# A mixture of experts whose rows are summed in DRAM by accumulating DMAs, and a second residual and layer norm done by halves

## The reference

```python
x = x + tanh(g_xattn[0]) * L0_xattn(layernorm(x), ctx)
x = x + tanh(g_ffn[0])   * L0_ffn(layernorm(x))
x = x + tanh(g_xattn[1]) * L1_xattn(layernorm(x), ctx)
x = x + tanh(g_ffn[1])   * L1_ffn(layernorm(x))

def L0_ffn(x):                      # a transformer layer with experts
    x = x + self_attention(rms(x) ...) @ wo
    h = rms(x, ff_ln_w)
    topv, topi = top_k(h @ wg, 4)   # of 16 experts
    weights = zeros.at[topi].set(softmax(topv))
    a = silu(h @ w1[e]) * (h @ w3[e])
    return x + sum_e weights[:, e] * (a @ w2[e])

def L1_xattn(x, y):                 # 16 heads of 32
    q = ln(x @ Wq + bq); k = ln(y @ Wk + bk); v = y @ Wv + bv
    ...                             # softmax(q k) v, and the same on the last 16 keys
    return ctx @ Wo + bo
```

## Time and profile before

| | |
|---|---|
| median of 3 runs | 2946.0 us (2941.17 to 2949.18) |
| the profiled execution | 2944.19 us, its span 2942.4 us |
| PE busy | 2398.4 us, 82% |
| DVE, ACT, POOL busy | 1768.0, 1472.8, 1100.9 us |
| mean granted clock of TensorE | 0.926 of full speed |
| DMA | 194.94 MB, mean 66 GB/s |

### The profile page before, as it was taken

One profiled execution on the slowest core, in us unless ns is written; L12 is line 12 of the kernel. 1 busy time (PEld: TensorE's weight loads), 2 busy tenths in 40 slices (PEclk: granted clock), 3 DMA queues, 4 the chain that ended last, 5 costly groups with the idle time before them and its releaser, 6 DMA issues. The chain is left out here.

```text
span 2942.4 us, 46079 instructions
## 1 busy us (share of the span) xinstructions
PE 2398.4 (82%) x14790; PEld 1995.1 (68%) x14790; DVE 1768.0 (60%) x3807; ACT 1472.8 (50%) x3030; POOL 1100.9 (37%) x1497
## 2 busy tenths in 40 slices
PE   5999999999957998899885649889860689999355
PEld 3778787878756888888873548888860577777232
DVE  3555555555554666666666625454535688888576
ACT  3444444444435666666653533333320587777543
POOL 0222222232313444444442555565633454444000
PEclk9999999999987999999996869999985799999788
DMA  3000000000010000000004654545546224241100
GB/s 108 19 17 12 7 18 11 18 7 18 0 29 11 19 18 18 18 18 18 18 1 136 207 171 168 174 161 170 169 130 177 79 61 108 61 107 65 75 8 22
DMA packets 124097, 194.94 MB, mean 66 GB/s; under 512 B 18736, under 2 KB 67120, under 8 KB 122224
## 3 DMA queue, kind: packets, MB, share of 16 engines
q1 hardware_dynamic: 109312, 157.50, 17.6%
q0 software_dynamic: 6640, 21.76, 2.3%
q10 hardware_dynamic: 8064, 14.68, 1.4%
HBM read 149.87 MB, written 44.04 MB: 66 GB/s over the span
## 5 line engine op out<-in xcount | busy, mean ns | idle before, releaser
L435 ACT ACTIVATE x_p<-x_p,x_least 128x1024 f32<-128x1024 f32 x128 | 147.3, 1151 | 307.3 <-DVE x_least L391 307.3
L1812 POOL TENSOR_TENSOR e_w<-e_raw,e_w 128x2048 fp32r<-128x2048 f32 x48 | 220.4, 4593 | 154.5 <-ACT e_w L1778 154.4
L375 DVE TENSOR_TENSOR x_pT<-pair,x_pT 128x512 fp32r<-128x512 f32 x256 | 164.3, 683 | 122.3 <-ACT x_pT L454 122.3
L469 POOL TENSOR_TENSOR x_carry<-x_rtotal 128x1 f32<-128x1 f32 x128 | 24.7, 193 | 559.8 <-DVE x_rtotal L368 559.8
L2143 PE MATMUL pair<-m_h,e_w 128*128 128x320 f32 x1536 | 230.5, 311 | 2.4 <-POOL e_w L1812 2.4
L2143 PEld LDWEIGHTS pair<-m_h,e_w 128*128 128x128 f32 x1536 | 229.0, 190 | 4.2 <-issue 2.8
L537 PE MATMUL pair<-x_pT,x_v 128*128 128x256 f32 x1536 | 209.5, 293 | 9.2 <-DVE x_pT L375 9.2
L537 PEld LDWEIGHTS pair<-x_pT,x_v 128*128 128x128 f32 x1536 | 193.9, 194 | 26.3 <-issue 18.3
L565 PE MATMUL pair<-x_kT,x_qT 128*128 128x512 f32 x768 | 206.9, 404 | 0.0
L993 ACT ACTIVATE s_p<-s_p,s_least 128x128 f32<-128x128 f32 (+3 forms) x256 | 143.6, 561 | 123.1 <-DVE s_least L903 122.9
L1131 PE MATMUL pair<-s_pT,s_v 128*128 128x256 f32 (+1 forms) x1152 | 158.8, 284 | 47.3 <-DVE s_pT L880 47.3
(11 more groups left out here) (337 smaller groups left out, 6079.6 us busy)
## 6 DMA issues: line engine op xcount, KB each, us to landing
e_raw<-in_L_ffn_w SPq DMA_DIRECT2D x48, 1024.0 KB
z_v<-z_vst SPq DMA_DIRECT2D x16, 768.0 KB, 3.4
y_rows<-hslot ACTq DMA_DIRECT2D x48, 256.0 KB, 4.7
z_kS<-z_k SPq DMA_DIRECT2D x24, 512.0 KB, 9.3
z_vS<-z_v SPq DMA_DIRECT2D x8, 1536.0 KB, 6.7
f_raw<-in_L_ffn_w SPq DMA_DIRECT2D x2, 4096.0 KB, 13.2
z_qS<-z_q SPq DMA_DIRECT2D x24, 256.0 KB, 4.2
s_wraw<-in_L_ffn_wq SPq DMA_DIRECT2D x9, 512.0 KB, 4.3
```

Of the source, the lines that this page charges most:

```text
L375: dve.tensor_tensor(pT[1][:, keys, q * P:(q + 1) * P], TR[j][:, :].rearrange("p (k n) -> p k n", n=P), pT[0][:, keys, q * P:(q + 1) * P].b ...
L435: act.activation(p[n][:, :], p[n][:, :], ACT.Exp, scale=-1.0, bias=least[:, n:n + 1], accum_out=total[:, n:n + 1]).then_inc(s_ex, 1)
L1812: pool.tensor_tensor(dst[1][:, :, :], raw[parity][:, :, :], dst[0][:, :, :].bitcast(F32), ALU.subtract).then_inc(s_lo, 1)
```

## The change

1. **Sums of the experts' rows.** `y_rows`, `where`, `share` and the rank and pick steps of the router go. y (residual and attention) is copied to a DRAM tensor `y_sum` of 1024 + 384 rows. The list matmuls now carry six columns for each token: its number in two parts, a one, and its gate in three bfloat16 parts. VectorE makes of them the gates of the list's places and target rows (unfilled places go to the extra rows). The down tile is scaled by its gate on its way out of PSUM into y's own buffer, and POOL adds it to `y_sum` by an indirect DMA with an add; each waits for the one before. After the last, two DMAs bring y back by halves.
2. **Second residual and norm by halves**, with the root of a half beside the other half's residual.
3. **Query weights** are loaded when the experts end, ahead of the two loads of y; the centring comes before the residual in VectorE's list. Keys and values of the second batch are loaded after the first batch's queries.
4. **Query low parts** go from VectorE to POOL.
5. **Key and value stage**: prologue and first steps come with later norm tiles (`RMS_FIRST` 6 for 3), and the low parts of odd key tiles go from POOL to VectorE.

The diff, cut to its core:

```diff
-                        if t < RMS_FIRST:
-                            kv["ACT0"](act, 2 * t)
-                            kv["ACT0"](act, 2 * t + 1)
-                        else:
+                        if RMS_FIRST - 3 <= t < RMS_FIRST:
+                            kv["ACT0"](act, 2 * (t - RMS_FIRST + 3))
+                            kv["ACT0"](act, 2 * (t - RMS_FIRST + 3) + 1)
+                        elif t >= RMS_FIRST:
                             kv["ACT"](act, t - RMS_FIRST)
...
-                        if rows and t in (1, RMS_FIRST):
+                        if rows and t in (RMS_FIRST - 2, RMS_FIRST):
                             kv["DVE0"](dve, t // RMS_FIRST)
...
+                if B <= u < len(units) and (u - B) % 2:
+                    n = u - B
+                    dve.wait_ge(s_fh, u + 1)
...
+                    dve.tensor_tensor(stlo[1][:, :, :], tt[u % 2][:, :, :], sthi[1][:, :, :].bitcast(F32), ALU.subtract).then_inc(s_fl2, 1)
...
-        RMS_FIRST = 3
-        kv_place = {"rms": range(0, NT - RMS_FIRST), "turned": range(5, 6), "picked": range(6, 7), "gated": range(7, 8), "after": range(8, 22)}
+        RMS_FIRST = 6
+        kv_place = {"rms": range(0, NT - RMS_FIRST), "turned": range(2, 4), "picked": range(4, 6), "gated": range(6, 7), "after": range(7, 22)}
...
+                sp.dma_start(y_sum[0:T, :].rearrange("(t p) d -> p t d", p=P), y3).then_inc(s_ysum, 16)
...
-                step(dve.tensor_copy(token[:, :, :], token32[:, :, :]))
+                step(dve.memset(token[:, NE:, :, 3:], 0.0))
+                step(dve.tensor_copy(token[:, :, :, 0:3], token32[:, :, :].unsqueeze(1).to_broadcast([P, NE + 2, NT, 3])))
+                step(dve.tensor_copy(token[:, 0:NE, :, 3], gate[:, :, :]))
+                step(dve.tensor_tensor(left[:, :, :], gate[:, :, :], token[:, 0:NE, :, 3], ALU.subtract))
+                step(dve.tensor_copy(token[:, 0:NE, :, 4], left[:, :, :]))
+                step(dve.tensor_tensor(left[:, :, :], left[:, :, :], token[:, 0:NE, :, 4], ALU.subtract))
+                step(dve.tensor_copy(token[:, 0:NE, :, 5], left[:, :, :]))
...
-                step(dve.tensor_tensor(row[:, :, :], placed, first[:, :].unsqueeze(1).to_broadcast([P, NT, NE]), ALU.add))
-
-                src = chosen
-                for k in range(4):
-                    n, dst = 1 << k, rank[k % 2]
-                    step(dve.tensor_copy(dst[:, :, 0:n], src[:, :, 0:n]))
-                    step(dve.tensor_tensor(dst[:, :, n:], src[:, :, n:], src[:, :, 0:NE - n], ALU.add))
-                    src = dst
-                step(dve.tensor_tensor(rank[0][:, :, :], src[:, :, :], chosen[:, :, :], ALU.mult))
-                for k in range(TOPK):
-                    for value, dst in ((row[:, :, :], row_k), (by_token, share)):
-                        step(dve.scalar_tensor_tensor(pick[:, :, :], rank[0][:, :, :], k + 1.0, value, ALU.is_equal, ALU.mult))
-                        step(dve.tensor_reduce(dst[:, k, :], pick[:, :, :], AX.X, ALU.add))
-                step(dve.tensor_copy(where[:, :, :], row_k[:, :, :]))
...
+                moe["query_weights"](sp)
+                sp.wait_ge(s_sum, 16 * CT * NE)
+                for k in range(2):
+                    sp.dma_start(y3[:, k * NT // 2:(k + 1) * NT // 2, :],
+                                 y_sum[k * T // 2:(k + 1) * T // 2, :].rearrange("(t p) d -> p t d", p=P)).then_inc(s_back[k], 16)
...
+                def scatter(e, s, r):
+
+                    pool.wait_ge(s_yd, CT * (e + 1) + r + 1)
+                    pool.wait_ge(s_tg, TARGET * (e + 1))
+                    if not (isinstance(e, int) and e == 0 and r == 0):
+                        pool.wait_ge(s_sum, 16 * (CT * e + r))
+                    n = 52 + CT * s + r
+                    pool.tensor_tensor(scrap[:, n:n + 1], eps[:, 0:1], eps[:, 0:1], ALU.mult)
+                    pool.indirect_dma_start(y_sum, bass.IndirectOffsetOnAxis(ap=target[s][:, r:r + 1], axis=0),
+                                            y3[:, CT * s + r, :], None, compute_op=ALU.add).then_inc(s_sum, 16)
...
                     gather(e + 1, 1 - s)
+                    if not first:
+                        scatter(e - 1, 1 - s, 0)
                     low(pool, w2, 3 * e + 3, s)
+                    if not first:
+                        scatter(e - 1, 1 - s, 1)
                     if not last:
                         low(pool, w1[1 - s], 3 * e + 4, (3 * s + 1) % 2)
+                    if not first:
+                        scatter(e - 1, 1 - s, 2)
+                    if not last:
                         low(pool, w3[1 - s], 3 * e + 5, (3 * s + 2) % 2)
...
-                for t in range(NT):
-                    if t >= 2:
-                        pool.wait_ge(s_add, TOPK * (t - 1))
-                    for k in range(TOPK):
-                        pool.indirect_dma_start(raw[t % 2][:, k, :], None, y_rows,
-                                                bass.IndirectOffsetOnAxis(ap=where[:, k, t:t + 1], axis=0)).then_inc(s_back[t % 2], 16)
...
+                    found = Y[0][:, 0:6 * CT].rearrange("p (r k) -> p r k", k=6)
+                    dve.tensor_copy(lists[s][:, :, :], found).then_inc(s_id, 1)
+                    dve.tensor_reduce(ids32[:, :], found[:, :, 0:2], AX.X, ALU.add).then_inc(s_id, 1)
...
+                    targets(e, s)
                     part_low(HC - 1)
                     listed(e + 2, s)
                     tokens(e + 1, 1 - s)
                     for r in range(CT):
-                        k = (CT * s + r) % 2
                         dve.wait_ge(s_y, CT * (e + 1) + r + 1)
-
-                        dve.wait_ge(s_st[k], (CT * 16) * i + 16 * ((CT * s + r) // 2 + (0 if k == (CT * s + r) % 2 else 1)) + 16)
-                        dve.tensor_copy(hslot[:, k * D:(k + 1) * D], Y[(r + 1) % 2][:, :]).then_inc(s_yd, 1)
...
+                        dve.tensor_scalar(y3[:, CT * s + r, :], Y[(r + 1) % 2][:, :], share[s][:, r:r + 1], None, ALU.mult).then_inc(s_yd, 1)
...
+                            tok = moe["token"][:, e, t, :] if isinstance(e, int) else (
+                                moe["token"][:, bass.ds(e, 1), t, :].rearrange("p e k -> p (e k)"))
+                            mm = pe.matmul(Y[0][:, 6 * r:6 * r + 6], mine[:, t, r * P:(r + 1) * P], tok,
                                            start=(t == 0), stop=(t == NT - 1))
...
+                inner_add(dve, 0)
+                inner_half(dve, 0)
+                inner_add(dve, 1)
+                inner_scale(dve, 0)
                 normal(0)
+                normal(1)
+                inner_half(dve, 1)
                 for s in range(STEPS):
-                    if s + 1 < NT:
+                    if s + 2 == QT:
+                        inner_scale(dve, 1)
+                    if s and s + 1 < NT:
                         normal(s + 1)
...
+                    if u >= 2:
+                        low(u - 2)
+                low(NT - 2)
+                low(NT - 1)
                 pool.wait_ge(s_lnh, 2 * NT)
```

More of the change, by code:

```diff
@@ L84, in program, with statistics @@
         s_stat, s_mv, s_std, s_rstd = [sem(f"ln_{n}") for n in ("stat", "mv", "std", "rstd")]
-        def statistics(n, before):
+        def statistics(n, before, more=0):
             def vector(dve):
@@ L1566, in route @@
             ones = sb("r_ones", [P, P])
-            first = sb("r_first", [P, NE])
-            token32 = sb("r_token", [P, NT, 2])
+            token32 = sb("r_token", [P, NT, 3])
             run = sb("r_run", [P, NT + 1, NE])
             pos = sb("r_pos", [P, NT, NE])
-            row = sb("r_row", [P, NT, NE])
-            rank = [sb(f"r_rank{i}", [P, NT, NE]) for i in range(2)]
-            pick = sb("r_pickm", [P, NT, NE])
-            row_k = sb("r_row_k", [P, TOPK, NT])
+            left = sb("r_left", [P, NE, NT])
             most = sb("r_most", [P, 1])
@@ L1737, in experts @@
                 ids = [few_only.enter_context(nc.sbuf_tensor(f"e_ids{i}", [P, CT], I32)) for i in range(2)]
+                moe["token"] = few_only.enter_context(nc.sbuf_tensor("e_token", [P, NE + 2, NT, 6], BF16))
+                moe["dummy"] = dummy = few_only.enter_context(nc.sbuf_tensor("e_dummy", [P, CT], F32))
+                lists = [few_only.enter_context(nc.sbuf_tensor(f"e_lists{i}", [P, CT, 6], F32)) for i in range(2)]
+                share = [few_only.enter_context(nc.sbuf_tensor(f"e_share{i}", [P, CT], F32)) for i in range(2)]
+                target32 = [few_only.enter_context(nc.sbuf_tensor(f"e_target32{i}", [P, CT], F32)) for i in range(2)]
+                target = [few_only.enter_context(nc.sbuf_tensor(f"e_target{i}", [P, CT], I32)) for i in range(2)]
             GU, Y = pairs[0:2], banks[4:6]
             s_in = [sem(f"e_in{i}") for i in range(2)]
-            s_mine, s_list, s_id, s_xt, s_xh, s_xl, s_got, s_add, s_done = [
-                sem(f"e_{n}") for n in ("mine", "list", "id", "xt", "xh", "xl", "got", "add", "done")]
```

(19 more changed lines are left out.)

170 lines of the change are left out of this document (96 added, 74 removed).

## The result

The changed kernel took 2949.33 us (median of 12 runs, 2946.98 to 2959.29), the kernel before beside it 2944.38 (12 runs, 2940.45 to 2949.18). The ratio is 1.0023, 95% interval 1.0013 to 1.0032: 5 us slower, where 2890 was forecast and the range ended at 2930. The profiled execution of the changed kernel took 2952.01 us, its span 2950.2, against 2942.4 before.

A forecast was written before the change was run, and what follows sets the result against it. TensorE was taken to bound the experts, and serial work without TensorE the 97.1 us after them. Terms -4 + 14 - 66.6 + 2.5 = -54 us from 2944.2 gave 2890, range 2858 to 2930.

The forecast's parts named there:

- Expert loop: List matmuls with six columns and register addresses: 0.9 us more an expert, x 16 = 14 us more; ends 0 and 22.
- Key and value stage: Shorter routing block against one more step behind it and a late prologue: 4 us less; ends 12 less, 6 more.
- rival 5: The reordered key and value stage loses 15 us or more by its late prologue: 2909; chance 0.02.
- The copy of y: 2 MB into DRAM on SP's queue ahead of the router's loads, wanted some 30 us later: costs nothing.
- Tail: Last expert to query projection: projection starts at 2220.7, not 2287.28, so 66.6 us less.
- Residual to projection: After the last expert: residual tiles, statistics, norm tiles and first low part before the projection, 12.9 us.
- POOL's lock on the residual: After the last expert, POOL's query weight split holds VectorE's residual until 2207.8 even if the sums come earlier.
- Scatters in the loop: Expert loop: three scatters take 3 x (0.65 + L) us, hidden in a 29.0 us expert while L is under 9.0.
- L: A scatter's time from issue to landing: taken as 4.7 us, bounded by 2.4 and 9.5.
- Rival 4: Scatters take over the expert loop: L = 10 leaves no gain, L = 13 gives 3095; chance 0.12 slower, 0.02 level.
- Target operations: Expert loop: six small VectorE operations, 1.2 us with hand-overs, ahead of the last low part: cost nothing.
- Query projection: Low parts moved to POOL delay its output bias, for which the attention waits: 2.5 us more; ends 0 and 5.

The follow-up runs named there:

- e4_lists_twice: Kernel before the change with each expert's 24 list matmuls done twice, same result, nothing else altered: 2984.9 us, ratio 1.0142.
- e8_plain_scatter: Changed kernel with the scatters writing their rows and not adding them: 2949.2 us, ratio 1.0027 to the kernel before.
- e10_all_disjoint: Changed kernel with all four mendings, each scatter waiting only for those of the expert before: 2878.51 us, ratio 0.9779 to the kernel before.

## Why the prediction was wrong

**Expert loop, +14 forecast, +37 measured: the step that failed.** The size of the list block was right (0.9 us more forecast, 0.75 measured, with one register operation for each distinct tile and no repeats). What failed is the silent rule that it costs its own time and no more. The block stands behind a wait of 2.9 us and ahead of full work, and made 0.75 us longer it keeps the clock low through turns and first down tile, in each expert; e4_lists_twice shows it without the rest of the change. The prediction's own row said that the clock was near an edge: a first down tile of 3.92 us, where the one at 1955.66 in the same timeline took 3.04, and half of the experts had such a fall. It had the mean clock of 0.97 before it and costed nothing. Why the list block, a few small matmuls behind a wait, tips the clock in some experts and a block twice as long in all of them, the runs don't show. The step is 23 of the 62 us between the sum (-54) and what the two profiles differ by (+8).

**Attention, nothing forecast, +18 measured: not in the sum.** VectorE's code ahead of the attention got longer and ScalarE's shorter, and with that both engines stood still at the loop's branch, twice. That the place of the code decides it is shown by moving it in both kernels; that they wait there for instructions is inferred from the fetch packets. Nothing of the change's work has to do with it.

**Key and value stage, -4 forecast, +12 measured.** The gain was about right in kind (2.6 us with the old places), the loss by the late prologue was given 6 us at most and measured 14.3. The prediction named the condition (a first step later than 1600: it came at 1612), and rival 5 had this late prologue, at 15 us or more and with 2 in 100. The wait that it didn't cost was VectorE's for the stores of the norm's rows, which the moved centring had covered. The copy of y, costed at nothing, cost nothing that moving it could win.

**Tail, -66.6 forecast, -61.4 measured: right in its steps.** Landing of an accumulating scatter: 4.7 forecast, 4.4 to 4.8 measured when alone, 7.3 for the one beside the load of the query weights. Half of y back: 6.2 and 5.7. Residual to projection: 12.9 and 12.5. The 5.2 us short are 1.9 of the last expert's list block and clock and 3.7 from its first copy to the residual, by the 7.3 and by the POOL operation of 1.70 us, with 0.4 given back behind it. POOL's lock on the residual did not show, because the sums came later; it showed as soon as they came earlier, at 3.6 us in e8_plain_scatter and 3.1 in e10_all_disjoint.

**Scatters in the loop: right.** They landed in 4.7 to 7.3 us, median 6.5 and not 4.7, and are hidden, as L stayed under 9. Rival 4, which held all the chance of slower, has no part in the result; the slowdown came from three losses, of which only the key and value stage's was among the rivals, with 2 in 100. **Target operations, costed at nothing**: right in the changed kernel, where the longer lists hid them; with short lists they and VectorE's copy cost 1.6 us an expert (29.84 against 28.28), through a cast that falls behind a POOL split. **Query projection**: 2.5 forecast, 0.9 measured, inside its ends.

The forecast's -54 was to be had: with its three misses mended the same design gives 2882.9, and 2878.5 with the three scatters of an expert side by side. Neither shows that the forecast was sound, since each needed code that the change didn't have.

## What to carry to other kernels

Read the granted clock stretch by stretch around every short block between two pieces of dense work, before adding to it: there 0.7 us cost 2.6, and taking it away paid as much. After any change of a long kernel, look at idle times without releaser where loops go round, also in stages that were not touched, and try the same kernel with dead code in a branch not taken; only with all engines' loops in a good place does it pay. Before work is moved off an engine's waits, list what those waits were for: they stay and are then bare.

## What the runs showed of the hardware that was not expected

- The clock: 0.7 us more of small matmuls behind a 2.8 us wait took an expert from 28.14 to 30.72 us, with or without the rest of the change. Before, the same loop took 27.4 us in one half of its experts and 28.8 to 29.0 in the other.
- A stall at a loop's branch, with instruction packets about it: 8 us for VectorE, 7 for ScalarE, twice, set by the place of the code alone. 2.25 MB of loads lay beside it; whether they lengthen it was not tried.
- An accumulating scatter of 128 rows of 2 KB takes POOL 1.62 us to issue, a plain one 1.01; alone it lands in 4.4 to 4.8 us, a plain one in 2.75; beside the 1 MB load of the query weights it took 7.3 and the plain one 3.87. Three that don't wait for each other, issued at 2185.1, 2187.0 and 2189.7, had all landed at 2199.4, 14.3 us; in a row they took 19.4.
- VectorE's cast of three elements waited 4.54 us for a POOL instruction over 2048 elements that began 0.06 us before it. The Trainium skill (SBUF — State Buffer, SBUF: two separate sides) has the two engines share a port pair as a lock held for a whole instruction; this trace agrees.
